# Where the diagonal matrices of B come from in a chunked selective scan

## The reference

```python
dA = jnp.exp(d_t[..., None] * A)
dBu = (d_t * u_t)[..., None] * b_t[:, None, :]
h = dA * h + dBu
y = jnp.einsum('bdn,bn->bd', h, c_t)
```

## Time and profile before

| | us |
|---|---|
| median of 3 runs | 5244.64 |
| the runs | 5246.55, 5226.87, 5244.64 |
| the profiled execution, its own time | 5233.07 |
| its span, first to last instruction | 5231.1 |
| VectorE busy | 3861.5 (74%) |
| GpSimd busy | 3782.1 (72%) |
| TensorE busy | 4528.0 (87%) |
| ScalarE busy | 3494.4 (67%) |
| mean granted TensorE clock | 0.965 |

### The profile page before, as it was taken

How to read it: one execution, slowest core, us unless ns; L and a number is a source line. 1 busy time by engine, 2 the same in 40 slices (tenths; PEclk the granted TensorE clock), 3 DMA queues, 4 the chain that set the end, 5 groups by cost and what they waited for, 6 DMA issues and landing times. The chain is left out here.

```text
span 5231.1 us, 88902 instructions
## 1 busy us (share of the span) xinstructions
PE 4528.0 (87%) x25304; PEld 3301.3 (63%) x25304; DVE 3861.5 (74%) x4157; ACT 3494.4 (67%) x6211; POOL 3782.1 (72%) x3035
## 2 busy tenths in 40 slices
PE   1688989898989898989898989889898998898998
PEld 0366666666666666666666666666666676586786
DVE  4598979888888888888888897979797998212211
ACT  1577777676767777777777776767676776563653
POOL 1388888888787888888878787878787899332322
PEclk9899999999999999999999999999999999999999
DMA  5202020202020202020202011020202020322313
GB/s 210 74 1 82 9 83 9 83 9 83 9 81 11 79 13 79 13 79 13 79 13 68 24 50 40 24 68 4 88 4 88 4 79 9 123 65 97 105 57 113
DMA packets 277100, 290.30 MB, mean 55 GB/s; under 512 B 87376, under 2 KB 166864, under 8 KB 274992
## 3 DMA queue, kind: packets, MB, share of 16 engines
q1 hardware_dynamic: 268080, 266.91, 16.2%
q10 hardware_dynamic: 8448, 16.78, 0.9%
HBM read 246.38 MB, written 37.26 MB: 54 GB/s over the span
## 5 line engine op out<-in xcount | busy, mean ns | idle before, releaser
L739 POOL TENSOR_TENSOR hc<-hs,c_rows 128x512 f32<-128x512 f32 x2048 | 2589.6, 1279 | 707.2 <-DVE hs L685 473.5
L775 PE MATMUL bank<-b_diag,du_t 128*128 128x128 f32 x9216 | 1285.2, 284 | 349.0 <-DVE hs L685 325.1
L685 DVE TENSOR_TENSOR_SCAN hs<-da,carry,bank 128x512 f32<-128x512 f32 x1152 | 1465.7, 1272 | 159.9 <-PE bank L775 85.8
L870 PEld LDWEIGHTS bank<-identity,hc 128*128 128x128 f32 x8192 | 1008.3, 143 | 707.3 <-issue 580.6
L775 PEld LDWEIGHTS bank<-b_diag,du_t 128*128 128x128 f32 x9216 | 1147.7, 196 | 430.5 <-DVE hs L685 391.4
L870 PE MATMUL bank<-identity,hc 128*128 128x128 f32 x8192 | 1232.8, 277 | 50.8 <-ACT sp_l L581 33.9
L685 DVE TENSOR_TENSOR_SCAN hs<-bank,carry,hs 128x512 f32<-128x512 f32 x896 | 1118.7, 1266 | 18.6 <-ACT bank L475 12.2
L475 ACT ACTIVATE da<-delta,neg_a 128x512 f32<-128x512 f32 x1152 | 822.7, 714 | 298.4 <-DVE hs L685 296.9
L475 ACT ACTIVATE bank<-delta,neg_a 128x512 f32<-128x512 f32 x896 | 612.2, 683 | 207.1 <-DVE hs L685 205.1
L670 DVE TENSOR_TENSOR hs<-bank,b_rows 128x512 f32<-128x512 f32 x768 | 520.4, 678 | 119.7 <-ACT carry L453 93.6
L856 PE MATMUL bank<-xs,w_out 128*128 (+1 forms) x1024 | 539.0, 631 | 67.7 <-issue 65.4
(11 more groups left out here) (159 smaller groups left out, 5909.9 us busy)
## 6 DMA issues: line engine op xcount, KB each, us to landing
c_rows<-b_and_c_rows SPq DMA_DIRECT2D x256, 256.0 KB, 7.3
xl<-x SPq DMA_DIRECT2D x48, 1024.0 KB, 5.5
b_diag<-b_diagonals SPq DMA_DIRECT2D x144, 256.0 KB, 7.2
b_rows<-b_and_c_rows SPq DMA_DIRECT2D x112, 256.0 KB, 7.1
c_rows<-in_x SPq DMA_DIRECT2D x8, 2048.0 KB, 8.4
xn<-in_x ACTq DMA_DIRECT2D x16, 1024.0 KB, 9.1
xres<-in_x SPq DMA_DIRECT2D x64, 256.0 KB, 3.2
x<-xres SPq DMA_DIRECT2D x64, 256.0 KB, 2.1
```

The lines of the kernel that those rows point to most:

```text
L685: dve.tensor_tensor_scan(hs[:, n % H_RING, :], decay, inflow, carry[:, STATE * j + n:STATE * j + n + 1], ALU.mult, ALU.add).then_inc(h_rea ...
L739: pool.tensor_tensor(hc[:, n % HC_RING, :], hs[:, n % H_RING, :], c_rows[:, n, :], ALU.mult).then_inc(hc_ready, 1)
L775: mm = pe.matmul(x_ps[ring_bank(nn)][:, q * P:(q + 1) * P], du_t[:, jn % 2, q * P:(q + 1) * P], b_diag[:, w, q, :], start=True, stop=True)
L870: mm = pe.matmul(y_ps[:, q * P:(q + 1) * P], hc[:, ns % HC_RING, q * P:(q + 1) * P], identity[:, :], start=ns == 0 and q == 0, stop=ns == ...
```

## The change

The DRAM buffer, its zeroing at the start (a memset of `b_diag` by GpSimd and a store of 2304 KB), the 9 element-wise stores a chunk and the 9 loads of 256 KB a chunk are gone, with their semaphores. In their place TensorE turns the four 32x128 blocks of `bc_rows` into the bank `pa` in slot 105 (four transposes), so that the values of B for 128 tokens stand in a column over the partitions. Then VectorE makes each diagonal matrix as the product of the identity with that column, spread over 128 columns: nine `tensor_tensor` of 128x512, one in each slot of tile 7 whose state is in `BY_TENSOR`, ahead of that slot's scan. For the chunk before the first, where nothing is scanned, the nine stand one after another. SP's loads of `b_rows` and `c_rows` now wait for the store of the rows alone.

```diff
--- before.py
+++ after.py
@@ -57,7 +57,7 @@
 TAP3, CONV, TANH, SILU = 2, 4, 5, 7
-X_MM, DBL, DT_SPLIT = (94, 95, 96, 96, 97, 98, 99, 100), 102, 104
+X_MM, DBL, DT_SPLIT, B_TURN = (94, 95, 96, 96, 97, 98, 99, 100), 102, 104, 105
...
@@ -240,9 +238,6 @@
                     sp.dma_start(neg_a[:, :, :], a_log).then_inc(weights_in, 16)
-                    sp.wait_ge(diag_blank, 1)
-                    sp.dma_start(diag_d.rearrange("w q (p c) -> p (w q) c", p=P),
-                                 b_diag[:, :, :, :].rearrange("p w q c -> p (w q) c")).then_inc(diag_zeroed, 16)
                     for i in range(BATCH * CT):
@@ -272,7 +267,6 @@
 
-                    pool.memset(b_diag[:, :, :, :], 0.0).then_inc(diag_blank, 1)
                     pool.wait_ge(w_in_loaded, 16)
...
@@ -409,17 +403,7 @@
                         sp.dma_start(bc_d, bc_rows).then_inc(bc_stored, 16)
-                        if not scan:
-                            sp.wait_ge(diag_zeroed, 16)
-                        for w, n in enumerate(BY_TENSOR):
-                            wait(sp, diag_loaded[w], 16 * f)
-                            settle(sp, sp_fence)
-                            sp.dma_start(diag_d[w:w + 1, :, 0:P * P:P + 1],
-                                         bc_rows[n:n + 1, :].rearrange("a (q p) -> a q p", p=P),
-                                         allow_slow_non_contiguous=True).then_inc(diag_stored, 16)
                         sp.wait_ge(bc_stored, 16 * (f + 1))
-                        settle(sp, sp_fence)
-                        sp.wait_ge(diag_stored, 16 * N_T * (f + 1))
                         settle(sp, sp_fence)
@@ -431,11 +415,6 @@
                                              bc_d[n:n + 1, :].partition_broadcast(P)).then_inc(b_loaded[v], 16)
-                            if n in BY_TENSOR:
-                                w = BY_TENSOR.index(n)
-                                wait(sp, dbu_mm, N_T * (JT * (c + 1) - 1) + w + 1)
-                                sp.dma_start(b_diag[:, w, :, :], diag_d[w].rearrange("q (p c) -> p q c", p=P)
-                                             ).then_inc(diag_loaded[w], 16)
                             wait(sp, hc_ready, STEPS * c + (JT - 1) * STATE + n + 1)
@@ -493,7 +472,7 @@
                                     wait(act, bc_stored, 16 * f)
-                                    wait(act, diag_stored, 16 * N_T * f)
+                                    wait(act, b_turned, f)
                                     wait(act, var_mm, CT * f + ct - 1)
@@ -654,6 +632,16 @@
                                              xres[:, ct % 2, :]).then_inc(x2_stat, 1)
+                            if front and j == JT - 1 and n in BY_TENSOR:
+
+                                w = BY_TENSOR.index(n)
+                                dve.wait_ge(b_turned, f + 1)
+                                wait(dve, dbu_mm, N_T * (tile if scan else 0) + (w + 1 if scan else 0))
+                                row = pa[:, 0:BLOCKS * 2 * STATE].rearrange("p (q r) -> p q r", q=BLOCKS)
+                                dve.tensor_tensor(b_diag[:, w, :, :],
+                                                  identity[:, :].unsqueeze(1).broadcast_to([P, BLOCKS, P]),
+                                                  row[:, :, n:n + 1].broadcast_to([P, BLOCKS, P]),
+                                                  ALU.mult).then_inc(diag_ready, 1)
@@ -769,18 +757,27 @@
                                 if jn == 0:
-                                    pe.wait_ge(diag_loaded[w], 16 * (cn + 1))
+                                    pe.wait_ge(diag_ready, N_T * cn + w + 1)
                                 wait(pe, h_ready, step + 3 - scans_before(nn) if scan else 0)
                                 for q in range(BLOCKS):
                                     mm = pe.matmul(x_ps[ring_bank(nn)][:, q * P:(q + 1) * P],
                                                    du_t[:, jn % 2, q * P:(q + 1) * P], b_diag[:, w, q, :], start=True, stop=True)
                                 mm.then_inc(dbu_mm, 1)
 
+                            if front and slot == B_TURN:
+                                pe.wait_ge(dt_split, f + 1)
+                                pe.wait_ge(xs_ready, JT * (f + 1))
+                                settle(pe, pe_fence)
+                                for q in range(BLOCKS):
+                                    mm = pe.transpose(pa[:, q * 2 * STATE:(q + 1) * 2 * STATE],
+                                                      bc_rows[:, q * P:(q + 1) * P],
+                                                      identity[3 * RANK:, 3 * RANK:])
+                                mm.then_inc(b_turned, 1)
                             if front and slot in MEAN:
                                 ct = MEAN.index(slot)
                                 pe.wait_ge(gn_applied, CT * f + ct + 1)
                                 if ct == 0:
-                                    wait(pe, xs_ready, JT * f)
+                                    wait(pe, diag_ready, N_T * f)
                                 mm = pe.matmul(pa[:, :], channel_mean[:, :], xn[:, f % 2, ct, :], start=ct == 0,
                                                stop=ct == CT - 1)
                                 if ct == CT - 1:
```

More of the change, by code:

```diff
@@ L212, in mamba_and_linear_attention @@
             consts = sem("consts")
-            diag_blank, diag_zeroed = sem("diag_blank"), sem("diag_zeroed")
             halved = sem("halved")
@@ L354, in mamba_and_linear_attention @@
             du_turned, du_t_ready, du_copied = sem("du_turned"), sem("du_t_ready"), sem("du_copied")
-            diag_stored, diag_loaded = sem("diag_stored"), [sem(f"diag_loaded{w}") for w in range(N_T)]
+            b_turned, diag_ready = sem("b_turned"), sem("diag_ready")
             dbu_mm = sem("dbu_mm")
```

1 line of the change is left out of this document (removed).

## The result

The changed kernel takes 5217.34 us (median of 9 runs, 5200.8 to 5228.2), the kernel before 5237.21 us on the same chip. The ratio is 0.9961 with a 95% interval of 0.9944 to 0.9977: 0.4% faster, less than the 0.5% that I had set as the bound for a change. The forecast was 5214, from a median of 5244.6 over three runs; over nine it is 5237.2, so in medians the gain was 19.9 us, not the 30.5 of the forecast. The profiled executions are 5233.07 and 5204.89 us, spans of 5231.1 and 5203.2 us. The sum stands close to the forecast, but two of its terms were far off in opposite directions, so the parts matter more than the total.

What follows compares the result with a forecast made beforehand. No engine paces throughout: tile 7 is GpSimd's, tile 0 TensorE's and ScalarE's. Terms -7 - 14.0 + 33 - 36 - 6.5 = -30.5 from the 5244.6 median give 5214 us; 0.82 between 5172 and 5264.

Steps and rivals of the forecast that it cites:

- Zeroing: Start, statistics phase: 2304 KB less DMA traffic moves all behind it forward, -7 us, bounds 0 and 11.3.
- First diagonals: Ahead of the first scan: TensorE no longer waits for stores and loads, only four transposes stand ahead, -14.0 us.
- Nine products: VectorE in tile 7: 0.6 us each, 5.4 a chunk less 3.2 of waits, +33 us over 15 chunks.
- the product is dear: Rival, chance 0.10: reading one PSUM column 128 times costs 1.19 us a product, total 5294, slower.
- cover: VectorE's 3.2 us of waits in tile 7, taken to absorb that much of the products' 5.4 us a chunk.
- no cover: Rival, chance 0.12: VectorE's waits in tile 7 move with it, all 5.4 us stay, 48 more, 5262.
- Transposes: Slot 105, tile 6: at most 1.1 us of TensorE, taken as 0; uncovered 17 us.
- DMA in tile 7: Nine fewer 256 KB loads leave the queue nearly empty for `xn`, so tile 0 shrinks 2.6 us a chunk, -36 us.
- early `xn` doesn't help: Rival, chance 0.12: last row loads still fill the engines at the jump, the L488 wait stays, 5250.
- Jump: Jump back of the loop: 0.5 us of the 4.9 us stand goes, -6.5 us over 13, bounds 0 and 31.
- A: Theory posed after the result: 256 KB transfers queued at the jump back delay the engines' code fetch there.

Runs made afterwards that it cites:

- twice_products: Changed kernel with eight of the nine products of a chunk made a second time, one slot later; 5284.83 us, ratio 1.0095 to the kernel before.
- no_products: Changed kernel with the diagonals made once, ahead of chunk 0, and used by all chunks (result not the reference's); 5162.57 us, ratio 0.9861.
- before_early_xn: Kernel before with the load of `xn` issued in slot 124, ahead of the jump, not slot 0; 5204.36 us against 5249.30, ratio 0.9919.
- late_products: Changed kernel with five products in tile 7 and the last four in slot 6 of the next tile 0; 5196.45 us, ratio 0.9924.
- copies_back: Changed kernel with nine unused 256 KB DRAM-to-DRAM copies a chunk on SyncE's queue, where the diagonals' loads stood; 5235.58 us, ratio 0.9999.
- rows_after_jump: Changed kernel with the last six row loads of each chunk issued behind the jump, once step 2 of the next tile 0 is done; 5165.88 us.

## Why the prediction was right, and where its steps were not

**Zeroing, -7.** Right for the statistics: their first instruction starts at 22.68 us in place of 29.60, 6.9 earlier. Of that 5.7 us reached the first scan when the store alone was moved, 3.9 in the changed kernel, where TensorE's granted clock on the way to `du` was 0.86 in place of 0.89. In the whole launch no gain of it could be measured.

**First diagonals, -14.0.** Right, 15.1: TensorE's wait fell from 15.80 to 0.69 us, and the four transposes took 0.4 us. With the zeroing the start moved by 18.9, where the sum was 21.

**Nine products, +33.** The price of 0.6 was right (0.58), so "the product is dear" is out: a column of PSUM repeated 128 times costs VectorE what a plain operand does. The mis-sized term is the cover: 48.4 us for 15 chunks is 3.2 each, so 2.0 of 5.2 were covered, not 3.2 of 5.4. I took all three waits as cover; 1.08 us of them stayed in chunk 2. With 48.4 us measured, 33 forecast and 81 with no cover, the term lay a third of the way to the rival "no cover". twice_products shows that nothing was left under a tenth product.

**Transposes, 0.** Right: tile 6 sums to 410.46 us without the products (no_products), to 410.36 before.

**DMA in tile 7, -36.** This step failed, in one half, and by the forecast's own sign: it was to be wrong if L488 still waits 2 us, and it waits 32.2 / 14 = 2.3. That tile 0 hinges on `xn` was right, and right in size: before_early_xn takes 42.4 us from it. That "the queue should be nearly empty when `xn` is asked for" was wrong: I judged the last microseconds of the tile by its mean, 220 GB/s over 27.4 us, while SP spreads the loads with the slots up to the jump and beyond it (973.82). The load still took 8.0 us in place of 9.1, its waits fell from 38.8 to 32.2, tile 0 by 11.0. That `xn` is asked for 2.0 us behind the last row and not 4.7 is not the reason: with longer stands no_products and late_products waited for it even more (35.4 and 34.2). What I had as the rival "early `xn` doesn't help" is for the most part what happened: the last row loads were still in the queue, though 11.0 of the 36 came.

**Jump, -6.5.** Mis-sized: 43.4, past the upper bound of 31. The 0.5 us was a choice, made by weighing a few remaining loads; the stand fell by 3.3. copies_back brings 36.0 of it back, and 17.3 of TensorE's 27.8, by traffic alone, so A holds for the stand; of the 54.4 us of jump and tile 0 together it explains only 11.8. The Trainium skill's rule of a forced DMA fetch ("Runtime: NRT & Kernel Launch", "Instruction fetch mechanics") pointed to the larger value, and the trace agrees as far as it goes: in the kernel before the first packets of kind "instruction" come over 2 us behind the last scan (none from 988.72 to 990.72, five in the 2 us after that), in the changed one the first comes within 1 us. no_products gives another 19.7 us of stand without more traffic, so the two causes overlap and don't add; as I read it, that part is VectorE arriving earlier, and tile 0 gives it back (jump plus tile 0 moves by 0.3, TensorE's stand by 3.1 in 13 jumps).

**The sum.** Jump and tile 0 together were forecast at -42.5 and came to -54.4; start and products (+12.0 forecast, +29.5 measured) were 17.5 us worse. The one nearly cancels the other but for 5.6 us. The rest, which the forecast did not have, gave 3.0 more (tile 1 -7.3 and tiles 2 to 5 -0.3, against +4.6 in chunk 0 and at the end), and the base was 7.4 us too high (5244.6 from three runs, 5237.2 from nine). So 5214 came near 5217 in part by luck: from 5237.2 the same sum gives 5207. I had given 0.58 to a gain over 0.5%, and 0.32 to none. The 0.5% bound lies inside the interval of the ratio, so between "faster" and "same" the measurement leaves it open.

**What stays open.** Why TensorE's clock stays up in tile 0 when the rows come later. In rows_after_jump, with a short stand of TensorE, it is 0.99 to 1.00 in all 14 tiles; but in the kernel before with its loads moved the stand is 55.6 us, and the clock is still 0.91 to 1.00 (0.87 to 0.96 in the unchanged kernel) and tile 0's busy time 20.0 us lower, so the short stand can't be all of it. What the nine stores do ahead of the nine loads, since neither was put back with the other. Which of the moved loads lets `xn` land sooner, the rows or `xres`. Which engine's code a packet carries: I could count them, not assign them.
